# Product with C on folded halves: two products of 128 and 64 rows in place of three

## The reference

```python
Bu = jnp.einsum('btd,nd->btn', u, B_w)
kernel = jnp.exp(t[:, None] * jnp.log(eig)[None, :])
...
h = jnp.fft.ifft(K_hat[None] * Bu_hat, axis=1).real[:, :seq_len, :]
y = jnp.einsum('btn,dn->btd', h, C_w) + D * u
...
x = x + _layernorm(_L0_attn_ref(_layernorm(x, axis=-1), ...), axis=-1)
x = x + _layernorm(_L0_ffn_ref(_layernorm(x, axis=-1), ...), axis=-1)
```

## Time and profile before

| | us |
|---|---|
| median of 3 runs | 1153.27 |
| lowest, highest | 1153.24, 1154.78 |
| the profiled execution | 1153.37 |
| its span, first to last instruction | 1151.4 |
| PE busy | 1133.6 |
| DVE busy | 915.2 |
| ACT busy | 703.7 |
| POOL busy | 622.4 |
| mean granted TensorE clock | 0.999 of 2.4 GHz |

### The profile page before, as it was taken

How to read it: one execution, slowest core, us unless ns; L and a number is a source line. 1 busy time by engine, 2 the same in 40 slices (tenths; PEclk the granted TensorE clock), 3 DMA queues, 4 the chain that set the end, 5 groups by cost and what they waited for, 6 DMA issues and landing times.

```text
span 1151.4 us, 16819 instructions
## 1 busy us (share of the span) xinstructions
PE 1133.6 (98%) x5102; PEld 928.9 (81%) x5102; DVE 915.2 (79%) x2002; ACT 703.7 (61%) x1370; POOL 622.4 (54%) x480
## 2 busy tenths in 40 slices
PE   8999999999999999999999999999999999999997
PEld 4777888888888888888888888888888888888885
DVE  6798877878888788877878778788887888778765
ACT  6675565655656565575655666566565655756564
POOL 1386564654556455464655556455464655556453
PEclk9999999999999999999999999999999999999999
DMA  4240212102021110212102021111212102020110
GB/s 129 69 128 1 75 37 65 46 20 65 28 74 38 47 43 23 74 37 66 46 12 73 28 75 37 47 38 28 74 38 66 46 6 78 28 72 30 47 51 15
DMA packets 82713, 57.61 MB, mean 50 GB/s; under 512 B 35360, under 2 KB 64192, under 8 KB 82624
## 3 DMA queue, kind: packets, MB, share of 16 engines
q1 hardware_dynamic: 82624, 56.54, 16.8%
HBM read 48.13 MB, written 8.39 MB: 49 GB/s over the span
## 4 chain that ended last, share of the span: by engine, by line
PE 96%; DVE 1%; ACT 1%; DMA 0%; issue 0%; POOL 0%; SPq 0%; POOLq 0%; DVEq 0%; ACTq 0%
PE g L280 10%; PE u L280 10%; PE u L282 10%; PE g L282 10%; PE u L281 10%; PE g L281 10%; PE y L280 10%; PE y L282 10%; PE y L281 10%; PE n_ps L287 2%; PE m_ps L280 1%; PE m_ps L282 1%; PE m_ps L281 1%; PE m_ps L372 1%; PE m_ps L371 1%
## 5 line engine op out<-in xcount | busy, mean ns | idle before, releaser
L1125 POOL TENSOR_TENSOR hid_lo<-hid,hid_hi 128x512 fp32r<-128x512 f32 x255 | 341.3, 1338 | 416.7 <-ACT hid_hi L574 416.5
L568 ACT ACTIVATE gate<-g 128x512 f32<-128x512 f32 x512 | 305.5, 597 | 326.7 <-PE g L282 325.1
L848 DVE TENSOR_TENSOR hid<-gate,u 128x512 f32<-128x512 f32 x512 | 348.5, 683 | 165.1 <-ACT gate L568 133.9
L574 ACT ACTIVATE hid_hi<-hid 128x512 fp32r<-128x512 f32 x512 | 321.1, 627 | 38.5 <-DVE hid L848 38.0
L854 DVE TENSOR_TENSOR hid_lo<-hid,hid_hi 128x512 fp32r<-128x512 f32 x257 | 210.7, 820 | 1.8
L280 PE MATMUL g<-xe_hi,w_hi 128*128 128x512 f32 x512 | 206.4, 403 | 0.1
L280 PE MATMUL u<-xe_hi,w_hi 128*128 128x512 f32 x512 | 199.9, 390 | 1.7 <-DVE hid L848 1.7
L280 PE MATMUL y<-hid_hi,w_hi 128*128 128x512 f32 x512 | 200.1, 391 | 0.3 <-ACT hid_hi L574 0.2
L282 PE MATMUL y<-hid_hi,w_lo 128*128 128x512 f32 x512 | 199.8, 390 | 0.0
L282 PE MATMUL g<-xe_hi,w_lo 128*128 128x512 f32 x512 | 199.7, 390 | 0.0
L281 PE MATMUL g<-xe_lo,w_hi 128*128 128x512 f32 x512 | 199.6, 390 | 0.0
(11 more groups left out here) (205 smaller groups left out, 1131.7 us busy)
## 6 DMA issues: line engine op xcount, KB each, us to landing
cw_b<-cw_scratch SPq DMA_DIRECT2D x128, 256.0 KB, 3.3
x_sb<-x_in SPq DMA_DIRECT2D x16, 256.0 KB, 3.1
out_scratch<-acc_t SPq DMA_DIRECT2D x60, 64.0 KB, 2.3
ffn<-out_scratch SPq DMA_DIRECT2D x15, 256.0 KB, 2.7
x_out<-o_sb SPq DMA_DIRECT2D x15, 256.0 KB, 2.2
stage<-wgate_in SPq DMA_DIRECT2D x8, 256.0 KB, 2.9
stage<-wup_in SPq DMA_DIRECT2D x8, 256.0 KB, 3.4
stage<-wdown_in SPq DMA_DIRECT2D x8, 256.0 KB, 4.2
```

The source lines that it names most:

```text
L568: nc.scalar.activation(gate[:, k % 2, :], g_ps[k % 2][:], ACT.Silu).then_inc(gate_ready, 1)
L574: nc.scalar.activation(hid_hi[:, k % RING, :], hid[:, k % RING, :], ACT.Copy).then_inc(hi_ready, 1)
L848: nc.vector.tensor_tensor(hid[:, k % RING, :], gate[:, k % 2, :], u_ps[k % 2][:], ALU.mult).then_inc(hid_ready, 1)
L1125: nc.gpsimd.tensor_tensor(hid_lo[:, k % RING, :], hid[:, k % RING, :], hid_hi[:, k % RING, :].bitcast(f32), ALU.subtract).then_inc(lo_pool, 1)
```

## The change

The product with C becomes two matmuls. DVE's last multiplication by `trig` writes both halves into `m_ps`; ACT copies the sine half (partitions 64 to 127) to `w_sin` on partitions 0 to 63; DVE adds it to the cosine half, which gives 64 rows in `v_sb`. The high part of these 64 rows is put in the upper half of `act_hi` (partitions 0 to 63), the low part in its lower half (64 to 127). One matmul of 128 rows with the doubled C high gives C high by high and C high by low at once; a second of 64 rows gives C low by high. The tables are moved to suit.

```diff
-TENSOR_AT = {"turn_cw": 4, "turn_x": 5, "bu": 9, "c": 15, "turn_y": 16, "turn_xe": 26,
+TENSOR_AT = {"turn_cw": 4, "turn_x": 5, "bu": 9, "c": 16, "turn_y": 17, "turn_xe": 26,
-SCALAR_AT = {"cw_t": 3, "hi_x": 8, "du": 8, "hi_w": 13, "fin_a": 19, "fin_b": 20, "z_a": 18, "z_b": 18,
+SCALAR_AT = {"cw_t": 3, "hi_x": 8, "du": 8, "move_sines": 13, "hi_w": 14, "fin_a": 17, "fin_b": 18, "z_a": 19, "z_b": 19,
-             "fin_turn": 6, "fin_stats": 14, "fin_var": 14, "fin_shift": 15, "leave": 12, "lo_w": 13, "y": 15, "stats_y": 16, "var_y": 16,
-             "shift": 18, "stats_x1": 22, "var_x1": 22, "shift_x1": 23, "lo_xe": 26, "softmax": 27, "exps": 30,
+             "fin_turn": 6, "fin_stats": 14, "fin_var": 14, "fin_shift": 15, "leave": 12, "fold": 13, "lo_w": 14, "y": 16, "stats_y": 17, "var_y": 17,
+             "shift": 19, "stats_x1": 22, "var_x1": 22, "shift_x1": 23, "lo_xe": 26, "softmax": 27, "exps": 30,
-GPSIMD_AT = {"rstd_x": 2, "fin_rstd": 15, "fin_add": 21, "rstd_y": 16, "residual": 18, "rstd_x1": 22}
+GPSIMD_AT = {"rstd_x": 2, "fin_rstd": 15, "fin_add": 21, "rstd_y": 17, "residual": 19, "rstd_x1": 22}
...
             def mix_c(c):
-                exact(m_ps[:], proj_hi[:, P:P + D], proj_lo[:, P:P + D], act_hi[:], act_lo[:]).then_inc(mixed_ready, 1)
+                nc.tensor.matmul(m_ps[:], proj_hi[:, P:P + D], act_hi[:], start=True, stop=False)
+                nc.tensor.matmul(m_ps[:], proj_lo[0:NS, P:P + D], act_hi[0:NS, :], start=False,
+                                 stop=True).then_inc(mixed_ready, 1)
...
+            def mix_move_sines(c):
+                act.wait_ge(parts_ready, c)
+                nc.scalar.activation(w_sin[:], m_ps[NS:P, :], ACT.Copy).then_inc(sines_moved, 1)
+
             def mix_hi_w(c):
                 act.wait_ge(w_ready, c + 1)
-                nc.scalar.activation(act_hi[:], v_sb[:], ACT.Copy).then_inc(act_hi_ready, 1)
+                nc.scalar.activation(act_hi[0:NS, :], v_sb[0:NS, :], ACT.Copy).then_inc(act_hi_ready, 1)
...
             def mix_leave(c):
-                nc.vector.tensor_tensor(v_sb[:], sum_sb[:], trig[:], ALU.mult).then_inc(w_ready, 1)
+                nc.vector.tensor_tensor(m_ps[:], sum_sb[:], trig[:], ALU.mult).then_inc(parts_ready, 1)
+
+            def mix_fold(c):
+                dve.wait_ge(sines_moved, c)
+                nc.vector.tensor_tensor(v_sb[0:NS, :], m_ps[0:NS, :], w_sin[:], ALU.add).then_inc(w_ready, 1)
...
-                nc.vector.tensor_tensor(act_lo[:], v_sb[:], act_hi[:].bitcast(f32), ALU.subtract).then_inc(act_lo_ready, 1)
+                nc.vector.tensor_tensor(act_hi[NS:P, :], v_sb[0:NS, :], act_hi[0:NS, :].bitcast(f32),
+                                        ALU.subtract).then_inc(act_lo_ready, 1)
```

More of the change, by code:

```diff
@@ L123, in build @@
         trig = sb("trig", [P, SEQ])
+        w_sin = sb("w_sin", [NS, SEQ])
         proj_hi, proj_lo = sb("proj_hi", [P, P + D], f32r), sb("proj_lo", [P, P + D], f32r)
@@ L158, in build @@
         xn_ready, xn_turned = sem("xn_ready"), sem("xn_turned")
+        parts_ready, sines_moved = sem("parts_ready"), sem("sines_moved")
         act_hi_ready, act_lo_ready, du_ready = sem("act_hi_ready"), sem("act_lo_ready"), sem("du_ready")
@@ L626, in body @@
                             mix_du(c + 1)
+                        if k == SCALAR_AT["move_sines"]:
+                            mix_move_sines(c + 1)
                         if k == SCALAR_AT["hi_w"]:
@@ L1027, in body @@
                             mix_leave(c + 1)
+                        if k == VECTOR_AT["fold"]:
+                            mix_fold(c + 1)
                         if k == VECTOR_AT["lo_w"]:
```

## The result

The changed kernel takes 1157.56 us (median of 7 runs, 1157.42 to 1157.86), the kernel before 1153.53 us (7 runs). The ratio is 1.0034, with a 95% interval of 1.0023 to 1.0046: 0.34% slower, where 0.29% faster was forecast, and outside the range of 1149.0 to 1155.0 us.

What follows compares the result with a forecast made beforehand. PE's instruction count times pace was taken as the bound: 3.40 us less, nothing added for row changes, stalls or chunk 0, took the profiled 1153.37 to 1149.97 us, so 1149.9 us (0.29% gain), range 1149.0 to 1155.0 us.

Steps and rivals of the forecast that it cites:

- What bounds the kernel: In steady chunks PE never runs dry; its number of instructions times their pace of 0.227 us sets the time.
- the 3.4 us saved: One of three matmuls with C goes in each of 15 chunks, 0.227 us each, 3.40 us in all.
- I take zero, nearest to the 0.04 us row: Changes between 128 and 64 rows on PE, 30 in all, cost nothing; 0.04 us each would be 1.2 us.
- the two upper bounds: Per change of rows on PE: 0.16 us if it runs empty (4.9 us), 0.35 with weights loaded after (10.5 us).
- the second rival: PE drains at each change of rows, then loads weights uncovered: 10.5 us more, 1160.4 us; chance 0.07.
- The row at the start: Trace start, 32-row to 128-row matmuls: starts 0.24, then 0.28 us apart, so a change of rows cost 0.04 us.
- So I add no stall: The chain behind C, a unit later, still meets PE at the turning and at `hid_lo` of unit 19: zero added.
- The third rival: Chain behind C overruns its margin if DVE's `hid_lo` meets POOL: PE waits 0.1 to 0.4 us a chunk; chance 0.15.
- The margin of 0.5 us at the turning: y ends at 489.4 and PE wants it for turning at 489.9; the margin was 0.7 us before.
- the margin of 0.5 us for `hid_lo` of unit 19: POOL's `hid_lo` ends at 499.4 and PE wants it at 499.9; the margin was 0.45 us before.
- Hidden work of ACT and DVE: ACT's added copies (9 us) and DVE's added additions (10 us), 19 us together, cost PE nothing.
- Chunk 0: First chunk, where 1.8 us are lost anyway: shifts by a unit counted as zero, up to 0.8 us either way.

Runs made afterwards that it cites:

- experiment 1: Changed kernel with its second product with C reading all 128 rows, the lower 64 weight rows being zero: 1157.93 us, ratio 1.0034 to the kernel before.
- Experiments 2 to 5: Kernel before with its third product with C on 64 rows, second and third on 64, third on 96, third on 32: 1159.58, 1159.54, 1153.83, 1159.52 us.
- experiment 3: Kernel before with its second and third product with C both on 64 rows, one behind the other: 1159.54 us (one run).
- experiment 6: Changed kernel with both products with C on 128 rows (zero weights), and `shift` on DVE moved from unit 19 to 18: 1152.37 us, ratio 0.9989 to before.
- experiment 7: Changed kernel, still with its 64-row product, with only `shift` moved to unit 18: 1155.51 us, ratio 1.0016 to the kernel before.

## Why the prediction was wrong, point by point

**What bounds the kernel, and the 3.4 us saved: right.** PE has 15 matmuls less, and where nothing else stands in the way (experiment 1, at the product) each is worth the pace of 0.227 us.

**"I take zero, nearest to the 0.04 us row": the step that failed.** A change between 128 and 64 rows costs 0.20 us, 0.40 a chunk, 15 x 0.40 = 6.0 us. It lies between the two upper bounds, 0.16 us (PE runs empty) and 0.35 us (and loads weights uncovered), and just above the 0.19 us from which the second rival had the kernel slower. That rival had the right sign, place and kind: the weight loads stand uncovered behind each change. Its price was nearly twice too high, since the wait ahead of the load is 0.09 us and not 0.16, and of the 0.188 us load only 0.11 show. The row at the start misled me. As I read it now, its products had one column each, so there was no stream of 512 columns for a change to interrupt, and the distance of 0.24 us for a single column already held latency; no run tests this reading. It would have been better to ask what the row could show at all, and to take the nearest row with a full stream, whose 0.16 us is close to the 0.20 measured. With the 6.0 us in the sum it would have said 1155.9 us; nearly all of the rest, up to the profiled 1157.8 us, belongs to the next step.

The Trainium skill was right on this: TensorEngine Tiling (Array Packing), section Tiling Modes, lists modes of 128, 64 and 32 rows and says that changing the mode drains the engine. Experiments 2 to 5 agree, by 0.40 us with 64 rows, 0.43 with 32 and 0.04 with 96, which fit only the mode of 128; that the array itself runs empty no trace here shows, only the weight loads held back. I set it against TensorE: Matmul & The Clock Gate, whose table at the end says that a single product of 32 rows takes as long as one of 128. That is no contradiction, as it speaks of the product and not of a change: in experiment 3 the second 64-row product took as long as a full one, and the changes cost 0.40 us all the same. For 32 rows no run measured a product by itself.

**"So I add no stall": wrong as well, and hidden by the first error.** In the changed kernel only 0.09 us a chunk show in units 22 to 25, and 1.0 us in chunk 0, because the 0.40 us give the other engines time. Without them (experiment 1) the chain behind C costs 0.50 us a chunk (69.504 less 69.234 - 0.227) and eats more than the whole gain. The third rival named the place and said 0.1 to 0.4 us; it was in force beside the second, where I had them as alternatives. The terms that were off, read in experiment 1:

- The low part first waits 0.17 us for ACT's `act_hi`. It then takes 1.02 us and not 0.68, as it reads two SBUF operands while POOL works; its mean is 1047 ns in the changed kernel, where all 15 meet POOL (before, 14 of 15 did not, at 679 ns). With both, `hid` of unit 15 starts 1.44 us after unit 16 does (488.42 less 486.98), where I had 0.74.
- I started y from the end of C. It is DVE's queue that sets it: `hid` of 15, `hid_lo` of 14, `hid` of 16 and the weighing come first, and y ends at 491.59, 0.6 us later than forecast in relation to PE. The margin of 0.5 us at the turning was -0.1.
- From there the lateness goes on by way of POOL. With y the variance and `rstd` are late, and with them POOL's `hid_lo` of unit 17 queued behind `rstd`: I had it end just before 494.7, by which it would have cleared DVE's `hid_lo` of unit 18; in relation to PE it ended 0.5 us later, and DVE's took 0.95 us instead of 0.68. That is the condition that the third rival named. Together with the 0.2 us that PE itself lost at the turning, `shift` and z came 0.6 us late, and the margin of 0.5 us for `hid_lo` of unit 19 was gone. Moving `shift` alone won back 0.37 us a chunk (experiment 6), which shows that z was the link.

**Hidden work of ACT and DVE: right in effect, off for DVE.** ACT's copy of the sines took 597 ns each and cost PE nothing. DVE gained 10.1 us for the additions, as forecast, but its total fell by 1.0 us. The largest term is `shift`, with 11.5 us less: before, 16 of its 49 instructions were issued while POOL worked (mean 1.01 us, the others 0.15), in the new order 2. `hid_lo` fell by another 6.0 us, and the low part of the product with C rose by 4.4.

**Chunk 0** moved by 1.0 us to the slow side, where 0.8 either way was allowed. It seems to hang on `shift` too: from the first g of chunk 0 to that of chunk 1 the traces have 73.29 us before, 74.43 in the changed kernel and 73.42 in experiment 7, where `shift` alone was moved. These are single traces.

Left open: whether the remaining 0.09 to 0.13 us a chunk over the ideal 69.00 can be won by another order. Not measured: the price of row counts between 64 and 96, and of a change between 64 and 32.

## What to carry to other kernels

A product on 64 rows (or 32) within a stream of 128-row products costs two interruptions, here 0.20 us each and nearly a whole 512-column matmul each; pad it with zero rows, which gave back the full pace here for one subtraction ahead of the loop. When the bound engine gets faster, every chain that was just in time must be walked again through each engine's queue, starting from what stands ahead of a step and not from when its data are ready. And read waits of a pipelined engine from distances of starts: here (experiment 1) 0.5 us a chunk were lost without the page's busy share or list of waits saying so.

## What the runs showed of the hardware that I had not expected

**A change of rows reaches past its neighbour.** It slows two distances, by 0.09 and 0.11 us, so one product of 64 rows disturbs three. The weight load behind a change is not made ahead: it starts 0.317 us after the matmul before it (0.427 at the change back, where that matmul had itself stood 0.11 us for its load), and not 0.003 us as in the stream.

**A tiny VectorE instruction takes as long as POOL's.** In experiment 6 `shift`, 4 elements from two SBUF operands, is issued just after POOL's `hid_lo`. The timelines of DVE and POOL:

```profile
493.30 1.25 DVE L708 SCALAR_TENSOR_TENSOR shift<-mv,rstd 128x4 f32<-128x4 f32 x1 [0.50 <-POOL rstd L1125]
```

```profile
493.24 1.28 POOL L1143 TENSOR_TENSOR hid_lo<-hid,hid_hi 128x512 fp32r<-128x512 f32 x1
```

It ends at 494.55, POOL's at 494.52; undisturbed it takes 0.15 us. The Trainium skill says it in GPSIMD Engine Reference, section Specifications: the SBUF interfaces are shared with VectorE, with contention for VectorE instructions that have two SBUF inputs. The rows agree, and add the size: the wait is for the rest of POOL's instruction, up to 1.1 us, whatever the length of one's own. In the trace of the kernel before, all 16 `shift` instructions that were issued while POOL worked ended 0.02 us after POOL's. `hid`, whose second operand is in PSUM, was not held: 0.68 us whether POOL worked or not. In hand-written orders like this one a small statistic can so be the costliest step of a chain.
